# Eight-bit layers and chosen tokens at the end of a four-layer megakernel: another order of the pieces

## The reference

```python
# expert layer "m2": 8 experts of 128 hidden features, the best 2 per token
out = sum(weight[e] * (silu(x @ w1[e]) * (x @ w2[e])) @ w3[e])
# eight-bit layers "q": per batch b, two of these with silu(gate) * up between
def _smooth_quant_linear(x, w):
    s = sqrt(max(amax_x, EPS) / max(amax_w, EPS)); s = max(s, EPS)
    xs, ws = x / s, w * s
    x_scale = max(max(abs(xs), axis=-1), EPS) / 127     # ws the same
    x_q = clip(round(xs / x_scale), -127, 127)          # w_q the same
    return x_q @ w_q.T * x_scale * w_scale.T
# chosen tokens "c": of each batch the 64 tokens with the largest router weight
weights = x @ W_r + b_r
h = gelu(take(x, topk_idx) @ W1 + b1)                   # 1024 hidden features
blk = h @ W2 + b2
out = scatter(blk * (weights * chosen)) + x * not_chosen
```

## Time and profile before

| | us |
|---|---|
| median of 3 runs | 1169.79 (1168.46 to 1172.9) |
| the profiled execution: its own time | 1173.39 |
| its span in the trace | 1171.8 |
| PE busy / DVE busy / ACT busy / POOL busy | 1030.5 / 744.2 / 483.9 / 257.5 |
| last expert steps, with the eight-bit layers of half 0 | 1009.8 to 1079.0 |
| eight-bit layers of half 1 beside the chosen tokens of half 0 | 1079.1 to 1138.9 |
| chosen tokens of half 1 and the last transfer | 1139.0 to 1171.8 |

### The profile page before, as it was taken

The page is one execution under the profiler, slowest core; times in us unless marked ns, Lnnn a source line. Parts: engine busy times, 40 slices in busy tenths (PEclk is TensorE's granted clock), DMA queues, the critical chain, the costliest instruction groups (busy, mean ns, idle before and its releaser), DMA issues.

```text
span 1171.8 us, 14115 instructions
## 1 busy us (share of the span) xinstructions
PE 1030.5 (88%) x4772; PEld 706.2 (60%) x4772; DVE 744.2 (64%) x1808; ACT 483.9 (41%) x1160; POOL 257.5 (22%) x206
## 2 busy tenths in 40 slices
PE   5766679999999999999999999999899989886736
PEld 2222233568999988899755556566566655444625
DVE  4888994335666667766745464567677655557553
ACT  3554452136666666666411112135455441132331
POOL 2445562121111112111000024502812100011110
PEclk9887889999999999999999999999999899898657
DMA  5000001010111131110012221220000003112000
GB/s 211 0 1 0 0 1 45 1 41 28 41 41 41 41 119 41 36 37 25 1 54 81 69 67 54 68 68 2 1 1 1 2 11 137 64 41 78 15 18 18
DMA packets 16335, 46.90 MB, mean 40 GB/s; under 512 B 2300, under 2 KB 3462, under 8 KB 15624
## 3 DMA queue, kind: packets, MB, share of 16 engines
q1 hardware_dynamic: 15400, 44.67, 11.8%
q10 hardware_dynamic: 864, 1.34, 0.3%
HBM read 44.96 MB, written 1.05 MB: 39 GB/s over the span
## 4 chain that ended last, share of the span: by engine, by line
PE 70%; DVE 8%; issue 5%; POOL 4%; ACT 2%; POOLq 0%; DVEq 0%; ACTq 0%
PE psum L1408 15%; PE psum L1427 6%; PE psum L905 5%; PE psum L1097 5%; PE psum L1108 5%; PE psum L1077 4%; PE psum L1647 4%; PE psum L766 4%; PE psum L908 3%; PE psum L1088 2%; PE psum L1946 2%; PE psum L929 2%; POOL arena L392 2%; PE psum L777 2%; PE psum L1930 2%
## 5 line engine op out<-in xcount | busy, mean ns | idle before, releaser
L1408 PE MATMUL psum<-xT,arena 128*128 128x512 f32 x400 | 186.5, 610 | 11.0 <-DVE arena L2439 3.6
L1408 PEld LDWEIGHTS psum<-xT,arena 128*128 128x128 f32 x400 | 76.5, 195 | 91.6 <-issue 90.0
L987 POOL TENSOR_TENSOR arena<-arena,mhalf 128x8 f32<-128x8 f32 x32 | 53.5, 1670 | 274.1 <-DVE arena L972 274.1
L1461 ACT ACTIVATE arena<-psum 128x512 f32<-128x512 f32 x50 | 29.7, 596 | 186.6 <-PE psum L1408 178.9
L1491 DVE TENSOR_TENSOR arena<-psum,arena 128x512 f32<-128x512 f32 x50 | 34.5, 691 | 113.1 <-PE psum L1408 110.5
L392 POOL TENSOR_TENSOR arena<-arena 128x512 f32<-128x512 f32 x64 | 82.4, 1309 | 79.0 <-DVE arena L694 76.2
L1209 DVE SCALAR_TENSOR_TENSOR X<-psum,arena,X 128x256 f32<-128x256 f32 x128 | 55.9, 479 | 68.0 <-PE psum L1108 68.0
L1427 PE MATMUL psum<-arena 128*128 128x256 f32 x400 | 95.2, 380 | 2.7 <-DVE arena L1491 2.7
L449 PE MATMUL psum<-arena,ident 128*128 128x512 f32 x128 | 77.5, 703 | 22.5 <-POOL arena L392 22.2
L1427 PEld LDWEIGHTS psum<-arena 128*128 128x128 f32 x400 | 75.4, 190 | 32.6 <-issue 21.9
L1503 DVE SCALAR_TENSOR_TENSOR X<-psum,arena,X 128x256 f32<-128x256 f32 x192 | 83.1, 479 | 7.1 <-PE psum L1427 6.7
(11 more groups left out here) (280 smaller groups left out, 1993.0 us busy)
## 6 DMA issues: line engine op xcount, KB each, us to landing
arena<-in_moe SPq DMA_DIRECT2D x50, 384.0 KB, 3.0
arena<-in_w SPq DMA_DIRECT2D x32, 384.0 KB, 3.0
arena<-in_w SPq DMA_DIRECT2D x2, 1024.0 KB, 6.6
arena<-in_gu SPq DMA_DIRECT2D x1, 1280.0 KB, 6.1
X<-in_x SPq DMA_DIRECT2D x2, 512.0 KB, 10.5
arena<-in_ctok SPq DMA_DIRECT2D x2, 512.0 KB, 6.5
arena<-in_fsideT SPq DMA_DIRECT2D x1, 1024.0 KB, 4.8
arena<-in_fside SPq DMA_DIRECT2D x1, 1024.0 KB, 7.0
```

Of the source, the lines that this page charges most:

```text
L1408: mm = nc.tensor.matmul(bank[b], m.W[:, slot, which, c * P:(c + 1) * P], k.xT[:, c, cols], start=c == 0, stop=c == DC - 1)
```

## The change

In half 0 and half 1 alike the first layer gets one more empty piece before the spreading of the scales (`at0 + 3` becomes `at0 + 4`, and so on to `at0 + 10`), and so does the second, which starts at 16: 28 pieces, 0 to 27. The eight-bit layers of half 0 start one point later (`later(1, ...)`), and `beside_points` takes the banks accordingly. The expert layer doesn't run what is left of them at its end (`drain=False`); that is handed to `then`. In the tail the chosen tokens of half 0 start six pieces after the eight-bit layers of half 1, and get empty pieces between their own: the hidden features are two pieces, with the gelu in two pieces after them, and one or two empty pieces stand before the second product's bias, the scatter and the last adds. What is computed is the same.

```diff
-def moe_pe(k, m, beside, points=1, begun=0, last=lambda: None):
+def moe_pe(k, m, beside, points=1, begun=0, last=lambda: None, drain=True):
...
-    rest(beside[1])
+    if drain:
+        rest(beside[1])
@@ quantised_pool
-        yield
-        yield
-        yield
+        for _ in range(4):
+            yield
         pool.wait_ge(*at("q_sB", l.n, h, 0))
@@ quantised_pe (ACT and DVE the same)
-        n, at0 = l.n, 3 if l.n == 1 else 15
+        n, at0 = l.n, 3 if l.n == 1 else 16
...
-        yield
-        yield
-        yield
-        one, two = pair(at0 + 3)
+        for _ in range(4):
+            yield
+        one, two = pair(at0 + 4)
...
-        features_of(l, "q_xq", l.xq, pair(at0 + 6)[0])
+        features_of(l, "q_xq", l.xq, pair(at0 + 7)[0])
@@ quantised_dve
         nc.vector.reciprocal(l.rs, l.sm).then_inc(*tick("q_rs", n, h))
         yield
-        one = pair(at0 + 3)[0]
+        yield
+        one = pair(at0 + 4)[0]
@@ chosen_act
     yield
+    yield
     for f in range(m.NF):
+        if f == 4:
+            yield
@@ chosen_dve
     a.then_inc(*tick("c_sel", h))
     yield
     yield
+    yield
     dve.wait_ge(*at("c_kept", h))
...
     yield
+    yield
+    yield
     dve.wait_ge(*at("c_out", h))
...
+    yield
     yield
     dve.wait_ge(*at("c_weight", h))
@@
+def then(first, n, part):
+
+    for i in itertools.count():
+        if next(first, first) is first and i >= n:
+            break
+        yield
+    yield from part
@@
 def beside_points(i):
-    return pair_of(i // 4)
+    return pair_of((i + 1) // 4)
@@ tensor_program (the other three the same)
+    first = later(1, quantised_pe(k, st.quantised, 0, beside_points))
     moe_pe(k, st.moe2, (moe_head_pe(k, st.moe2, 1, beside_points),
-                        quantised_pe(k, st.quantised, 0, beside_points)), 4, begun=2)
-    rest(both(quantised_pe(k, st.quantised, 1, beside_chosen), chosen_pe(k, st.chosen, 0, beside_quantised)))
+                        first), 4, begun=2, drain=False)
+    rest(both(quantised_pe(k, st.quantised, 1, beside_chosen),
+              then(first, 6, chosen_pe(k, st.chosen, 0, beside_quantised))))
     rest(chosen_pe(k, st.chosen, 1, beside_quantised))
```

More of the change, by code:

```diff
@@ L1 @@
 from contextlib import ExitStack
+import itertools
 import concourse.bass as bass
@@ L1449, in moe_pe, with moe_act @@
         step(beside[st // m.total])
-    rest(beside[1])
-def moe_act(k, m, beside, points=1, last=lambda: None):
+    if drain:
+        rest(beside[1])
+def moe_act(k, m, beside, points=1, last=lambda: None, drain=True):
     nc, act, at, tick, bank, tag = k.nc, k.act, k.s.at, k.s.tick, k.bank, m.tag
@@ L1478, in moe_act, with moe_dve @@
         step(beside[st // m.total])
-    rest(beside[1])
-def moe_dve(k, m, nxt, beside, points=1, last=lambda: None):
+    if drain:
+        rest(beside[1])
+def moe_dve(k, m, nxt, beside, points=1, last=lambda: None, drain=True):
     nc, dve, at, tick, bank, tag = k.nc, k.dve, k.s.at, k.s.tick, k.bank, m.tag
@@ L1525, in moe_dve, with moe_pool @@
         step(beside[st // m.total])
-    rest(beside[1])
-def moe_pool(k, m, beside, points=1):
+    if drain:
+        rest(beside[1])
+def moe_pool(k, m, beside, points=1, drain=True):
     for st in range(m.steps):
@@ L2315, in quantised_pe @@
         pe.wait_ge(*at("q_made"))
-        features_of(l, "q_xq", l.xq, pair(at0 + 6)[0])
+        features_of(l, "q_xq", l.xq, pair(at0 + 7)[0])
         yield
         yield
-        one, two = pair(at0 + 8)
+        one, two = pair(at0 + 9)
         features_of(l, "q_wq", l.wq, one)
@@ L2325, in quantised_pe @@
         for i in range(2):
-            b = pair(at0 + 9)[i]
+            b = pair(at0 + 10)[i]
             k.bank_ready(b)
@@ L2375, in quantised_act @@
             act.wait_ge(*at("q_hid", 1, h, 1))
-        nc.scalar.copy(l.sB[:, 0:2 * l.F], bank[pair(at0 + 3)[1]][:, 0:2 * l.F]).then_inc(*tick("q_sB", n, h, 0))
+        nc.scalar.copy(l.sB[:, 0:2 * l.F], bank[pair(at0 + 4)[1]][:, 0:2 * l.F]).then_inc(*tick("q_sB", n, h, 0))
         yield
@@ L2380, in quantised_act @@
         yield
-        turned(l, "q_xq", l.XQT, pair(at0 + 6)[0])
+        turned(l, "q_xq", l.XQT, pair(at0 + 7)[0])
         yield
@@ L2384, in quantised_act @@
         yield
-        turned(l, "q_wq", l.WQT, pair(at0 + 8)[0])
+        turned(l, "q_wq", l.WQT, pair(at0 + 9)[0])
         act.wait_ge(*at("q_wr", n, h))
         act.wait_ge(*at("q_ws", n, h))
-        nc.scalar.copy(l.sB, bank[pair(at0 + 8)[1]]).then_inc(*tick("q_sB", n, h, 1))
+        nc.scalar.copy(l.sB, bank[pair(at0 + 9)[1]]).then_inc(*tick("q_sB", n, h, 1))
         yield
@@ L2840, in scalar_program @@
         later(4, begun(lambda: moe_left(k, k.act, st.moe1), moe_head_act(k, st.moe2, 0, beside_attention2)))))
+    first = later(1, quantised_act(k, st.quantised, 0, beside_points))
     moe_act(k, st.moe2, (moe_head_act(k, st.moe2, 1, beside_points),
-                         quantised_act(k, st.quantised, 0, beside_points)), 4)
+                         first), 4, drain=False)
     rest(both(quantised_act(k, st.quantised, 1, beside_chosen),
-              begun(lambda: moe_left(k, k.act, st.moe2), chosen_act(k, st.chosen, 0, beside_quantised))))
+              then(first, 6, begun(lambda: moe_left(k, k.act, st.moe2), chosen_act(k, st.chosen, 0, beside_quantised)))))
     rest(chosen_act(k, st.chosen, 1, beside_quantised))
@@ L2879, in gpsimd_program @@
         later(4, begun(lambda: moe_left(k, k.pool, st.moe1), moe_head_pool(k, st.moe2, 0)))))
-    moe_pool(k, st.moe2, (moe_head_pool(k, st.moe2, 1), quantised_pool(k, st.quantised, 0)), 4)
+    first = later(1, quantised_pool(k, st.quantised, 0))
+    moe_pool(k, st.moe2, (moe_head_pool(k, st.moe2, 1), first), 4, drain=False)
     rest(both(quantised_pool(k, st.quantised, 1),
-              begun(lambda: moe_left(k, k.pool, st.moe2), chosen_pool(k, st.chosen, 0))))
+              then(first, 6, begun(lambda: moe_left(k, k.pool, st.moe2), chosen_pool(k, st.chosen, 0)))))
     rest(chosen_pool(k, st.chosen, 1))
```

8 lines of the change are left out of this document (5 added, 3 removed).

## The result

The changed kernel takes 1158.55 us (median of 6 runs, 1156.74 to 1161.52) against 1172.2 for the kernel before on the same chip (6 runs); the ratio is 0.9885 [0.9859, 0.9911]. That is faster, by 13.65 us where 6.1 were forecast. The time lies inside the range, near the case of *more*; the gain doesn't. The range was set from a median of 1169.79 for the kernel before and so stood for gains of 0.8 to 12.8 us, and the six runs put that kernel 2.4 us higher. The profiled spans are 1155.3 and 1171.8.

The account below looks back on a forecast made before the run. Matmuls on PE bound most of the kernel, but in the last 160 us the chain through all engines does. Expert steps 4.2 plus tail 1.9 made 6.1 us, giving 1163.7 us; range 1157.0 to 1169.0.

Parts of the forecast that it names:

- more: Rival: expert-step waits too short to slow the clock (2.8), no hold (1.1), gather at full clock (1.9); 1157.9 us, chance 0.12.
- A: Expert steps 9 to 15: every eight-bit piece of half 0 at least a point later; 4.2 us earlier.
- B: Tail: another merging order of half 1's eight-bit layers and half 0's chosen tokens; 1.9 us earlier.
- step 9: Expert stage: gate 10 goes ahead of the turn; cost 7.4 us before, 3.5 after, gain 3.9.
- steps 10 and 11: Expert stage: 4.5 us of waits and slow clock before, 4.6 after; gain 0, the gaps only moved.
- to the product: Tail, from the scaling of the tokens to the product between the layers: 24.4 us before, 25.7 after; -1.3.
- to the scaling in layer 2: Tail, from the product between the layers to layer 2's scaling: 4.3 us before, 9.2 after; -4.9.
- The rest: Tail: four adds of the chosen tokens, 1.67 us, land in the chain; -1.7.
- Only A: Rival: only the expert steps gain, the tail's chain ends where it did; 1165.6 us, chance 0.14.
- only B: Rival: in the expert steps a wait replaces the one removed, only the tail gains; 1167.9 us, chance 0.12.
- Slower by clock: Rival: slow clock after three expert-stage waits (5.2 more) and in the tail's block (8.9 more); 1177.8 us, chance 0.10.
- Table load: Tail, ACT: silu's table load of 1.28 us leaves the chain; by the skill's 2.66 that step would be 1.4 better.

Follow-up runs that it names:

- all seven kernels with this stage: Seven profiled kernels that have the changed kernel's expert stage; the gate after step 9's wait took 1.88 us in all seven.
- B alone: Tail of the change with half 0's eight-bit layers ordered as before, against the kernel before: 1170.16 us, ratio 0.9963.
- the kernel with only the point: The change without half 0's added empty pieces, keeping its shift by one point, against the kernel before: 1157.07 us, ratio 0.9866.
- the extra matmuls: Matmuls with unread products in PE's waits, cut to size, plus early reductions; with two more groups, against the kernel before: 1145.76 us, ratio 0.978.
- each part alone: Only the expert-step half of the change, then only the tail half, each against the kernel before: ratios 0.9939 (1167.32 us) and 0.9963 (1170.16 us).

## Why the prediction was right, and where it was not

Both signs were right, and both sums were too small: A 4.2 against 6.7, B 1.9 against 6.3. That the time fell inside the range is in part luck: the kernel before measured 2.4 us slower in six runs than in the three that the forecast started from. By step, as gains:

| step | forecast | measured | from |
|---|---|---|---|
| step 9 | 3.9 | 5.5 | 7.4 less 1.89 |
| steps 10 and 11 | 0 | -2.0 | 4.5 less 2.68, 1.19, 2.19 (5.86 for 3.67) and 0.40 (1.01 for 0.61) |
| between the layers | 1.7 | 1.7 | no waits |
| layer 2 | 0.3 | 0.4 | 1.93 less 0.90 and 0.64 |
| the end | -1.7 | -1.5 | A less what PE gained up to its last product (8.2) |
| not in the sum | | 2.6 | |
| front of the tail | 9.8 | 9.6 | 17.54 less 7.99 |
| to the product | -1.3 | +1.8 | 24.37 less 22.55 |
| to the scaling in layer 2 | -4.9 | -4.4 | 4.26 less 8.65 |
| the rest | -1.7 | -0.7 | 13.75 less 14.44 |

**The waits were right, the clock behind them was not.** All five waits forecast for A came within 0.3 us. After step 9's the sum put 1.6 of slow clock, and there was none; after those of steps 10 and 11 it put 1.2, and there were 2.6 (2.6 to 2.7 in all seven kernels with this stage). The two misses nearly cancel. B alone and the kernel with only the point show that the same wait can be followed by either.

**The term that A lacked.** My sum counted waits of 0.35 us and more, and nothing else. PE's waits in the stage add up to 12.4 before and 7.3 after, where I had listed 11.65 and 7.3: 0.75. And a stop costs more than its wait: a group that waits for nothing starts some 0.16 us ahead of the modelled end of the one before (1012.16 against 1010.43 + 1.89), and eight matmuls take 3.67 behind a stop and 3.60 without. That is about 0.23 for each stop and, with some six fewer, 1.4 as an estimate. The remaining 0.4 may be the spreading of the scales behind the wait of 2.16, which took 1.00 before (1039.92) and 0.60 after (1037.63) and is in neither list.

**The middle of the tail.** This step had the wrong sign, by 3.1. To the end of the router's row I had 12.1 us, with both roundings ahead of it, and a hold of 1.1; the second rounding came behind it, and the product took 3.00, partly at full clock, not 3.75: 11.1 with the hold. The counting, with that rounding in it, took 4.0 instead of 3.1. The positions and the eight-bit product had 3.0 by half-clock rows; at full clock 1.7 passed. From the gather to the product between the layers 6.4 became 5.7. The hold on DVE was sized well (1.1 forecast, 1.43 - 0.17 = 1.26). The rows of before had shown the tail's router product, positions and gather at half clock, and I carried that over; the extra matmuls show how much hangs on it: with the clock at 1.00, 4.4 us in the tail (52.9 to 48.5) and 4.5 behind it (31.95 to 27.42), in an unchanged order of the real work.

**The rest.** The 1.67 of the four adds are there. I left out that the hold of 0.55 on DVE in layer 2 goes too; 0.2 more came from a turn at full clock (0.38 for 0.58), and 0.2 is open. Behind P2, where I had no change, 0.8 was gained by the same work at a higher clock: 0.40 for 0.60, 0.67 for 1.06 and 3.84 for 4.25 in the transposes of the row, the turn of the selection and the hidden features. Why the clock stood higher there is not shown.

**Rivals.** *Only A* and *only B* fall: each part alone is faster with an interval below 1. *More* comes nearest with 1157.9, for one of its three reasons (the gather's clock, 0.4 of 1.9); its other two, no slow clock in A and no hold, did not happen. *Slower by clock*: hidden features (3.84), second product and scatter ran at full clock. The Trainium skill (TensorE: Matmul & The Clock Gate, HAM oscillation) tells of a kernel in which each burst of matmuls starts at the low clock, after waits of about 3 to 5 us. The waits here were shorter, 0.6 to 2.7 us in stage A, and the clock fell after some (5.86) and not after others (step 9 and layer 2). **Table load:** the forecast booked 1.28 as gone from the chain; bringing it back costs 0.33, since in the new order silu isn't on the chain.

## What to carry to other kernels

Before costing a moved step, look for a long wait in an in-order queue and ask what stands behind it: here one 7.1 us wait of DVE for a product of the other chain held up the eight-bit weights, and a few empty pieces removed it nearly as well as the large shift did, as far as the rows tell. Where short matmuls alternate with other engines, price a stop at its wait plus a refill, and treat the clock as a resource of its own; idle reductions earlier and unread matmuls inside the waits gave nearly as much again as the change itself, but a group that overruns its wait gives it all back.

## What the runs showed of the hardware

- The granted clock after a wait of some 2 us is not fixed by the instructions up to there: 1.88 us in seven kernels and 3.50 in an eighth for the same four matmuls after waits of 1.89 and 1.90, and 1.95 and 3.56 after waits of 1.93 in two others. In the eighth it stood at 1.00 for 1.1 us behind the wait and fell to 0.53 while PE worked.
- Unread matmuls inside the waits held the granted clock at 1.00 from P1 to the end, where it was 0.73 and 0.77 without them (0.72 and 0.77 in the change).
- A tiny DVE operation (4 elements a partition) was held for 1.26 us by a POOL operation of 2.34 us, and two on 256 elements together for 2.0 us; a reduction that ran beside it was not held.
- What lies ahead of P0 varied by up to 6.6 us between profiled executions of kernels whose instructions there are the same, which is about as large as either part of the change.
